# Expert weights loaded in place and split by the Scalar and Vector engines, the slot products cut in two, the spike terms and the first A x V moved: a perceiver block on one core

## The reference, cut to what matters

```python
x = x + cross_attention(layernorm(x), ctx, mask, Wq, Wkv, Wo, qn_w, kn_w)
# self block, per sequence of 32 tokens:
Q, K, V = (sigmoid(4 * (batchnorm(xn @ W) - 1)) for W in (Wq, Wk, Wv))
t_Q, t_K = 1 - mean(Q), 1 - mean(K)
d = t_Q - t_K.T
A = where(d < 0, f, -f) + 0.9        # f = 0.9 * exp(-|d| / 0.5)
x = x + A @ V @ Wo + bo
# experts: 8 of them, the best 2 per token; w1, w3 (8, 512, 256), w2 (8, 256, 512)
scale = top-2 of softmax(xn @ gate_w)
x = x + sum_e (silu(scale * xn @ w1[e]) * (scale * xn @ w3[e])) @ w2[e]
```

## Time and profile before

| what | us |
| --- | --- |
| median of 3 runs | 832.8 (831.76, 832.80, 837.01) |
| the profiled execution, its own time | 832.88 |
| its span, from the first to the last instruction | 831.1 |
| PE busy in 200 to 300 us, cross attention | 100.00 of 100 |
| PE busy in 580 to 600, z stage | 15.78 of 20 |
| PE busy in 620 to 630, AO stage | 7.27 of 10 |
| PE busy in 670 to 680, routing | 3.62 of 10 |
| PE busy in 740 to 760, slot loop | 20.00 of 20 |

### The profile page before, as it was taken

One profiled execution on the slowest core, in us unless ns is written; L12 is line 12 of the kernel. 1 busy time (PEld: TensorE's weight loads), 2 busy tenths in 40 slices (PEclk: granted clock), 3 DMA queues, 4 the chain that ended last, 5 costly groups with the idle time before them and its releaser, 6 DMA issues.

```text
span 831.1 us, 13413 instructions
## 1 busy us (share of the span) xinstructions
PE 742.9 (89%) x4437; PEld 646.0 (78%) x4437; DVE 542.2 (65%) x1022; ACT 492.6 (59%) x1078; POOL 263.9 (32%) x184
## 2 busy tenths in 40 slices
PE   5899999999999999999999977999798728999960
PEld 3688899999999998989999966787577627788840
DVE  6876786868867768677686767634655563544532
ACT  4766785867767767678576663453274324566540
POOL 2561221212121212122121144626647122656530
PEclk9999999999999999999999999899998958999995
DMA  9831212111212212121213041120217652666658
GB/s 307 62 111 39 76 44 72 56 58 41 73 38 76 76 38 76 38 76 38 66 48 119 9 111 55 67 87 9 93 63 232 225 192 73 111 109 112 105 72 304
DMA packets 60039, 75.97 MB, mean 91 GB/s; under 512 B 8768, under 2 KB 33344, under 8 KB 60000
## 3 DMA queue, kind: packets, MB, share of 16 engines
q1 hardware_dynamic: 52544, 59.21, 23.8%
q0 software_dynamic: 5152, 12.06, 8.2%
q10 hardware_dynamic: 2304, 4.20, 1.4%
HBM read 54.75 MB, written 20.71 MB: 91 GB/s over the span
## 4 chain that ended last, share of the span: by engine, by line
PE 77%; DVE 9%; DMA 5%; ACT 4%; POOL 2%; issue 2%; SPq 1%; DVEq 0%; POOLq 0%; ACTq 0%
PE pK L32 35%; PE pV L32 12%; PE pP L32 10%; PE pS L32 6%; PE pT L1453 3%; PE pT L1634 3%; PE pP L1617 2%; DMA fin<-total 1%; PE pT L1739 1%; DMA total<-big,idx 1%; DVE a_flat L1226 1%; DMA big<-x_rows,idx_x 1%; PE pS L1688 1%; DVE bst L939 1%; DMA bn_vec<-in_L_attn_vv_dram 1%
## 5 line engine op out<-in xcount | busy, mean ns | idle before, releaser
L32 PE MATMUL pK<-parts 128*128 128x512 f32 x840 | 213.0, 402 | 7.9 <-POOL parts L512 7.9
L481 POOL TENSOR_TENSOR parts<-big,parts 128x1024 fp32r<-128x1024 f32 x32 | 77.4, 2418 | 340.7 <-ACT parts L710 340.7
L32 PEld LDWEIGHTS pK<-parts 128*128 128x128 f32 x840 | 153.9, 190 | 37.3 <-POOL parts L512 8.4
L32 PE MATMUL pK<-w,lhs 128*128 x276 | 71.2, 408 | 1.4 <-DVE lhs L1381 1.1
L32 PEld LDWEIGHTS pK<-w,lhs 128*128 128x128 f32 x276 | 51.9, 195 | 12.7 <-issue 2.6
L1402 DVE TENSOR_TENSOR w_p<-big,w_p 128x1024 fp32r<-128x1024 f32 x23 | 28.2, 1225 | 51.1 <-ACT w_p L902 48.7
L981 DVE TENSOR_TENSOR kn<-pK,head_rs 128x512 f32<-128x512 f32 x62 | 42.7, 688 | 20.1 <-ACT head_rs L612 19.5
L32 PE MATMUL pS<-kT,qblk 128*128 128x258 f32 x384 | 52.4, 287 | 2.0 <-DVE qoT L1015 2.0
L738 ACT ACTIVATE pT<-pP 128x512 fp32r<-128x512 f32 x32 | 19.1, 598 | 56.8 <-PE pP L1617 56.8
L32 PE MATMUL pP<-pT,parts 128*128 128x256 f32 x384 | 51.9, 284 | 0.0
L32 PEld LDWEIGHTS pS<-kT,qblk 128*128 128x128 f32 x384 | 49.1, 193 | 2.3 <-DVE qoT L1015 2.3
(11 more groups left out here) (273 smaller groups left out, 1597.6 us busy)
## 6 DMA issues: line engine op xcount, KB each, us to landing
big<-in_ctx_dram SPq DMA_DIRECT2D x32, 512.0 KB, 3.8
big<-in_L_ffn_w_dram SPq DMA_DIRECT2D x24, 512.0 KB, 4.8
total<-zero SPq DMA_DIRECT2D x32, 256.0 KB, 3.9
fin<-total SPq DMA_DIRECT2D x8, 512.0 KB, 7.2
big<-in_L_xattn_Wkv_dram SPq DMA_DIRECT2D x2, 1024.0 KB, 10.8
x_rows<-xn ACTq DMA_DIRECT2D x8, 256.0 KB, 2.3
total<-big ACTq DMA_DIRECT2D x8, 256.0 KB, 2.8
out_dram<-fin SPq DMA_DIRECT2D x4, 512.0 KB, 6.5
```

The costliest lines, as they stand in the source:

```text
L32: last = pe.matmul(out, lhs(a, c), rhs(b, c), start=start and c == first and n == 0, stop=stop and c == chunks - 1 and n == 2)
L481: nc.gpsimd.tensor_tensor(ctxN[:, u, LO], ctx_raw[:, u], ctxN[:, u, HI].bitcast(F32), ALU.subtract).then_inc(cn_lo, 1)
```

## The change

- **Layout.** Each expert's w1 and w3 land where its low part will be (`w13_raw[e]`), and the low part is written over them. For this `xT` moves to 64 KB, the self block's weights to their own `w_a` at 96 KB, `xn3` into the region of `w_raw` and `a_flat` over `bn_vec`.
- **Loads.** SP loads experts 0 and 1 behind the second set of `bn_vec`, 2 behind the third, 3 when 16 tiles of z are through, 4 to 6 when all of z is, 7 behind the last product with Wo. All of w2 is loaded at once when x and its normed copy are stored.
- **Splits.** POOL does none for the experts. ACT makes the high parts of 0, 1, 2 at n = 4, 6, 8, of 3 at n = 20, of 4 to 6 in halves at s = 1 to 6, of 7 after the routing. DVE makes the low parts of 0, 1, 2 at n = 6, 8, 10, of 3 at n = 22, of 4 to 6 in quarters, two in each of s = 2 to 7, of 7 in quarters in the first four slots.
- **Spike terms.** The diagonal matrices are written by ACT, two at each of n = 10 to 13; `ones` holds 1/512, so that the factor is in the product, which PE does right behind `z_product(15)`. d and |d| come at n = 17, exp at n = 18, A at n = 19 and 20.
- **First A x V** ahead of `z_product(23)`, its split at n = 22 and 23.
- **Routing.** The 24 row values get their own 16 products (24 columns), and `idx_x` is made ahead of the gates', which follow with 48 columns. POOL gathers before it waits for `zeroed` and `x2_out`.
- **Slot loop.** The last two results are copied into `xg`'s buffers, without the wait for a scatter; the last split of w2 comes behind that slot's hidden tile; the expert's number is loaded ahead of the waits.

```diff
...
-        a_flat = at("a_flat", [P, 2 * D], 60 * KB)
-        xT = at("xT", [P, 2, C, TILES * P], 96 * KB, F32R)
-        xn3 = at("xn3", [P, TILES, D], 112 * KB)
+        a_flat = at("a_flat", [P, 2 * D], 128 * KB)
+        xT = at("xT", [P, 2, C, TILES * P], 64 * KB, F32R)
+        w_a = at("w_a", [P, 2, 2, C, D], 96 * KB, F32R)
+        xn3 = wide[:, 0:2 * C * D].rearrange("p (t d) -> p t d", t=TILES)
...
+        w13_raw = [at(f"w13_raw{e}", [P, C, D], (2 * e + 1) * 8 * KB) for e in range(E)]
...
+        p_slot = pV1[:, 0:NJ]
+        p_gates = pP_flat[:, 0:2 * NJ].rearrange("p (v j) -> p v j", v=2)
...
+            return y_sb[:, j % 2, :] if j < NS - 2 else xg[:, j % 2, :]
...
+            def load_expert(e):
+                if e >= 4:
+                    sp.wait_ge(w13_hi, e - 3)
+                for lo, w in ((0, w1), (F, w3)):
+                    sp.dma_start(w13_raw[e][:, :, lo:lo + F], chunked(w[e])).then_inc(w13_in[e % 4], 16)
...
                 if w == 1:
-                    load_weight("av", "aq")
-
+                    sp.wait_ge(o_mm, 2 * TILES)
+                    load_expert(0)
+                    load_expert(1)
+            sp.wait_ge(xo_mm, TILES)
+            load_expert(2)
+            load_weight("av", "aq")
             load_weight("ao", "ak")
...
+            sp.wait_ge(z_c, 2 * TILES)
+            load_expert(3)
+            sp.wait_ge(z_mm, 3 * TILES)
+            for e in (4, 5, 6):
+                load_expert(e)
+            sp.wait_ge(ao_mm, TILES)
+            load_expert(7)
...
+            sp.wait_ge(xn_out, 16 * TILES)
...
-                if e >= 4 and e % 2 == 0:
-                    sp.wait_ge(w13_last, e // 2 - 1)
...
-            nc.gpsimd.memset(ones[:, :], 1.0)
+            nc.gpsimd.memset(ones[:, :], 1.0 / D)
...
-            for i in range(6):
-                w13_low(i)
...
                 gather(j)
+            pool.wait_ge(zeroed, 16 * B)
+            pool.wait_ge(x2_out, 16 * TILES)
...
+            def w13_high(e, part=slice(0, C)):
+                act.wait_ge(w13_in[e % 4], 32 * (e // 4 + 1))
+                act.activation(w13[:, e, HI, part], w13_raw[e][:, part], ACT.Copy).then_inc(w13_hi, 1)
...
+                if n in (4, 6, 8):
+                    w13_high(n // 2 - 2)
+                if TILES + 2 <= n < TILES + 6:
+                    for t in (2 * (n - TILES - 2), 2 * (n - TILES - 2) + 1):
+                        act.wait_ge(bn_c, 3)
+                        act.activation(a_all[:, t, :], ident[:, :], ACT.Copy, scale=rows[:, 0, t:t + 1]).then_inc(t_act, 1)
+                if n == 3 * TILES - 4:
+                    w13_high(3)
                 if n == 3 * TILES - 2:
-                    w13_high(0)
-                if n == 2 * TILES + 4:
-                    act.wait_ge(t_step, TILES + 4)
+                    self_high(0)
+                if n == 2 * TILES + 2:
+                    act.wait_ge(t_step, 4)
                     act.activation(a_flat[:, :], a_flat[:, :], ACT.Exp, scale=-1.0 / TAU).then_inc(t_act, 1)
...
-                if s < 5:
-                    w13_high(s + 1)
+                if 1 <= s <= 6:
+                    w13_high(4 + (s - 1) // 2, slice(2 * ((s - 1) % 2), 2 * ((s - 1) % 2) + 2))
...
-            w13_high(6)
             w13_high(7)
...
+                if 2 <= j < NS - 2:
                     act.wait_ge(added[j % 2], 16 * (j // 2))
-                act.activation(y_sb[:, j % 2, :], pY[j % 2], ACT.Copy).then_inc(y_set, 1)
+                elif j >= 2:
+                    act.wait_ge(xg_t, NS)
+                act.activation(y_of(j), pY[j % 2], ACT.Copy).then_inc(y_set, 1)
...
+                if i == NS:
+                    w2_high(NS - 1)
...
+                if i < NS - 1:
...
+            def w13_low(e, part=slice(0, C)):
+                dve.wait_ge(w13_hi, e + 1 if e < 4 else 11 if e == 7 else 2 * e - 4 + part.start // 2 + 1)
+                tt(w13[:, e, LO, part], w13_raw[e][:, part], w13[:, e, HI, part].bitcast(F32),
+                   ALU.subtract).then_inc(w13_last if e == 7 else w13_lo, 1)
...
-                    for r in range(TILES):
-                        ts(a_all[:, r, :], ident[:, :], rows[:, 0, r:r + 1], 1.0 / D, ALU.mult,
-                           ALU.mult).then_inc(t_step, 1)
                     ts(rows[:, 1, :], rows[:, 1, :], 1.0 / D, None, ALU.mult).then_inc(t_step, 1)
-                if n == 2 * TILES + 4:
+                if n == 2 * TILES + 1:
 
                     dve.wait_ge(t_pe, 1)
-                    dve.wait_ge(t_step, TILES + 1)
+                    dve.wait_ge(t_step, 1)
                     for g in range(2):
...
+                    dve.wait_ge(t_step, 3)
                     stt(a_all[:, :, :], dt_all[:, :, :], -1.0, dt_all[:, :, :], ALU.mult, ALU.max).then_inc(t_step, 1)
...
+                if n == 2 * TILES + 3:
+
+                    dve.wait_ge(t_step, 4)
                     ts(dt_all[:, :, :], dt_all[:, :, :], 0.0, 2 * A_STDP, ALU.is_lt, ALU.mult).then_inc(t_step, 1)
-                    dve.wait_ge(t_step, TILES + 5)
-                    dve.wait_ge(t_act, 1)
+                    dve.wait_ge(t_step, 5)
+                    dve.wait_ge(t_act, TILES + 1)
                     stt(dt_all[:, :, :], dt_all[:, :, :], -A_STDP, a_all[:, :, :], ALU.add, ALU.mult).then_inc(t_step, 1)
-                    dve.wait_ge(t_step, TILES + 6)
+                if n == 2 * TILES + 4:
+
+                    dve.wait_ge(t_step, 6)
                     stt(dt_all[:, :, :], dt_all[:, :, :], W_OFF, same_seq[:, :].unsqueeze(1).broadcast_to([P, TILES, P]),
...
+                if n in (6, 8, 10):
+                    w13_low(n // 2 - 3)
+                if n == 3 * TILES - 2:
+                    w13_low(3)
+                if n == 3 * TILES - 1:
+                    self_low(0)
...
+                if 2 <= s < TILES:
+                    for c in (2 * (s % 2), 2 * (s % 2) + 1):
+                        w13_low(4 + (s - 2) // 2, slice(c, c + 1))
...
-            routed(tt(tile_val[:, :, :, :], tile_hot[:, :, :].unsqueeze(2).broadcast_to([P, TOP_K * TILES, 3, NJ]),
-                      r_val[:, :, :].bitcast(F32).unsqueeze(3).broadcast_to([P, TOP_K * TILES, 3, NJ]), ALU.mult), val_set)
+            routed(tt(tile_val[:, :, 0, :], tile_hot[:, :, :],
+                      r_val[:, :, 0].bitcast(F32).unsqueeze(2).broadcast_to(pairs), ALU.mult), val_set)
...
+            gates = [P, TOP_K * TILES, 2, NJ]
+            routed(tt(tile_val[:, :, 1:3, :], tile_hot[:, :, :].unsqueeze(2).broadcast_to(gates),
+                      r_val[:, :, 1:3].bitcast(F32).unsqueeze(3).broadcast_to(gates), ALU.mult), val_set)
...
+            dve.wait_ge(i_mm, 1)
+            routed(tt(idx[:, :], p_slot, slot_row[:, :], ALU.add))
+            after_step()
+            routed(ts(idx_x[:, :], idx[:, :], T - 1, None, ALU.bitwise_and), idx_set)
...
-            dve.wait_ge(i_mm, 1)
-            routed(tt(idx[:, :], p_slot[:, 0, :], slot_row[:, :], ALU.add))
-            after_step()
-            routed(ts(idx_x[:, :], idx[:, :], T - 1, None, ALU.bitwise_and), idx_set)
-            routed(nc.vector.tensor_reduce(gate_of[:, :], p_slot[:, 1:3, :].rearrange("p v j -> p j v"), AX.X, ALU.add), idx_set)
+            dve.wait_ge(i_mm, 2)
+            routed(nc.vector.tensor_reduce(gate_of[:, :], p_gates.rearrange("p v j -> p j v"), AX.X, ALU.add), idx_set)
...
-            w13_low(6)
-            w13_low(7)
...
+                if i == NS:
+                    w2_low(NS - 1)
+                if i < C:
+                    w13_low(E - 1, slice(i, i + 1))
...
+                if n == 3 * TILES - 1:
+                    pe.wait_ge(t_step, 7)
+                    self_product(0)
...
-                if n == 2 * TILES + 1:
-                    pe.wait_ge(t_step, TILES)
+                if n == 2 * TILES - 1:
+                    pe.wait_ge(t_act, TILES)
...
-                last = pe.matmul(p_slot, row_hot[:, k, :], tile_val[:, k], start=k == 0, stop=k == pairs - 1)
+                last = pe.matmul(p_slot, row_hot[:, k, :], tile_val[:, k, 0, :], start=k == 0, stop=k == pairs - 1)
+            last.then_inc(i_mm, 1)
+            pe.wait_ge(val_set, 4)
+            for k in range(pairs):
+                last = pe.matmul(p_gates, row_hot[:, k, :], tile_val[:, k, 1:3, :], start=k == 0, stop=k == pairs - 1)
             last.then_inc(i_mm, 1)
...
-                    pe.wait_ge(w13_lo, 6)
-                    pe.wait_ge(w13_last, 2)
+                    pe.wait_ge(w13_lo, 4 + 3 * C)
+                if j == E:
+                    pe.wait_ge(w13_last, C)
...
```

117 lines of the change are left out of this document (39 added, 78 removed).

## The result

| | before | after |
| --- | --- | --- |
| median of 5 runs | 832.46 us (831.44 to 837.01) | 810.85 us (806.96 to 813.14) |
| ratio, 95% interval | | 0.973 [0.9691, 0.977] |
| profiled execution, its span | 831.1 | 805.2 |

The forecast was 811.5, with a range of 806 to 820. Each boundary is a row of the profile; a stretch is the difference of two.

The account below looks back on a forecast made before the run. PE's waits between the K tiles and the routing were taken as mostly DVE held up by POOL. Savings of 16.0 (z gap and AO stage), 2.0, 2.3 and 1.0 made 21.3 off 832.9: 811.6, stated as 811.5, range 806 to 820.

Parts of the forecast that it names:

- The z gap: Behind `z_product(15)`: three z products and the product by `ones` fall from 17.2 us to 9.8, saving 7.4.
- The AO stage: From the z gap to the routing: 10.6 us of waits and slow products regained, less 2.0 of new costs.
- Routing: From the routing's first step to `idx_x`: narrower index products bring `idx_x` 2.0 us earlier, bounds 0.8 and 2.6.
- Gathers: Second gather, no longer beside w2's loads, lands in 4.7 instead of 7.02: 2.3 us saved, bounds 0 and 2.7.
- First slots: First four slots: DVE's extra quarter against its value load moved off the path, together taken as 0.
- SP's queue: SP's expert loads around the third `bn_vec` and in the z stage: four more megabytes, costed at nothing.
- The end: Last slots: 0.7 us from making `hT` before the last w2 split, 1.0 with the copy's scatter wait; bounds 0 and 2.6.
- DVE as the bound: AO stage: DVE sets the pace, six tiles take 6.0 instead of 4.97, +6 us, 817.5; chance 0.13.
- POOL still holding DVE: Low part at n = 10 and four terms of A held up beside POOL's work: 814.5; chance 0.10.
- Gathers sharing with w2: The gathers still share with w2's loads, so the 2.3 us is lost: 814; chance 0.12.
- A late load: ACT waits at a `w13_high` ahead of a sigmoid; one transfer of about 5 us shows once: 816.5; chance 0.06.
- a clock that stays down: Short waits keep PE at 1.2 GHz over the AO stage and 20 us more: 841, slower than before; chance 0.03.

Follow-up runs that it names:

- diag_dve1: Changed kernel with the eight diagonal matrices back on DVE, the product by `ones` behind `z_product(17)` and the terms of A one tile later: 817.33 us.
- pool_low1: Changed kernel with the low parts of experts 4 to 6 made whole by POOL in the AO stage instead of DVE's quarters: 810.67 us.
- sp_late: Changed kernel with the loads of expert 2 and Wv held back until the third `bn_vec` set has landed: 808.82 us, ratio 0.9705 to before.
- best: Changed kernel with `sp_late`'s wait, expert 7's low part whole ahead of the first `x_low`, and unread products in PE's idle time: 808.05 us, ratio 0.9699.
- again1: The changed kernel profiled and timed once more with no edit: 811.28 us, span 809.4.
- warm1: Changed kernel with unread products added in PE's idle time: three before the members, six before the `row_hot` products, two before the first slot's transposes: 808.72 us.

## Why the prediction was right, point by point

The time, 811.5 against 810.85, and the sum, 21.3 against a difference of 21.6 between the medians, are right. The mechanism on which 16.0 of the 21.3 rest, PE waiting for a DVE that POOL holds up, is right too. Of the seven terms the z gap is right, the AO stage right in size with its condition misnamed, the end right in sum with its parts exchanged; the other four miss in both directions and cancel.

- **The z gap, 7.4.** Measured 7.2, and `diag_dve1` puts it back. The product by `ones` took 1.88 and no wait was in front. DVE's terms of A, costed at 0.5, did grow beside POOL (1.83, 2.12 and 1.72, where `diag_dve1` has 1.30, 1.23 and 1.22, the last two with POOL quiet) and were hidden. POOL was held in its turn: its eight adds of bo took 11.51 in place of 9.92.
- **The AO stage, 10.6 less 2.0, with the gap 16.0.** Measured 16.6 and 14.9. The wait for the first `lhs2` is 1.03 for 1.1; the wait of 1.64 for the last tile is there to the digit; tiles are 4.97 to 5.0. The 0.4 and the 0.5 don't show. What the forecast didn't see is that the wait of 1.64 can bring the clock down behind it, which makes 1.7 between two profiles of one kernel. And its sentence "POOL is out of the AO stage now, so the 3.88 goes back to 0.55" names the wrong condition. POOL may stay, as `pool_low1` shows, if its pieces don't meet a norm.
- **Routing, 2.0.** Measured 0.84, at the lower bound of 0.8. The step that failed is "between a third of 0.226 and the whole of it, I take 0.12, near the lower end because the weight load stays". If the weight load is the reason, the upper end follows from it and not the lower: 24, 48 and 72 columns cost 3.59, 3.59 and 3.62. The 0.84 is nearly all DVE's smaller product ahead of them, 1.36 to 0.56.
- **Gathers, 2.3.** Measured 4.4. The cause named, w2's loads beside them, is right and is worth 4.2 alone. The term was mis-sized in two places: the second gather, taken at 4.7, lands in 3.6 (659.91 to 663.5), and its start behind `idx_x` comes 1.3 sooner, since POOL's first gather takes 1.28 in place of 2.59. That 2.59 stood in the earlier trace rows and wasn't asked about; it is DVE's hold on POOL.
- **First slots, 0.** 1.0 to 1.3 were gained: the clock is back at 1.00 in the window of 668 to 670, 3 us after the first product's start, where before it was 0.82 in the window that begins 4 us after it; the product takes 4.41 or 4.14 in place of 5.20. Not all of it is the change's: in the nine profiles whose gathers run as here that product takes 3.93 to 4.94. The 0.7 to 0.9 of the later slots are two slots that took 5.51 and 5.01 before, where the others take 4.8.
- **SP's queue, 0.** 1.2 lost at the third `bn_vec`, shown by `sp_late`. "Their condition is met earlier" was true of experts 0 and 1; the loads that did harm are those right behind the third `bn_vec`.
- **The end, 1.0.** Measured 1.07, with the parts exchanged: 0.7 for the order is 0.1, and the buffers, for which 0.3 was left, are 1.1. PE's earlier end alone buys nothing, since the copy then stands at the scatter.
- **The rivals.** DVE as the bound: out, since taking a third of its work away (`pool_low1`) gains nothing. POOL still holding DVE: seen in the terms of A, hidden. Gathers sharing with w2: not here, but `best` shows that it was 2 us away. A late load, and a clock that stays down: no. The 841 of that rival is a slip in the sum: by its own words, 39.8 us become 80, it is over 851.
- **The signs.** The product by `ones`, the first `lhs2`, the tiles, the norms (0.55 at most) and the second gather are as forecast. The clock of 1.00 up to the routing is so in the first profile and not in `again1`. The first slot's product is 23.0 us earlier than 688 there and 18.1 in `again1`, whose part ahead of the z gap took 1.9 longer than before; so that sign asked for more than the change decides.

Forecast too high were the routing by 1.2, the queue by 1.2 and, in `again1`, the stage by 1.1; too low were the gathers by 2.1 and the slots by some 2. That the sum came out within a microsecond was luck in its parts.

## What to carry to other kernels

Between DVE and GpSimd ask not how much work they share but what meets what: in these traces an operation that reads PSUM or takes statistics passes, a norm from SBUF to SBUF waits until GpSimd's piece ends, a gather's issue on GpSimd waits until DVE's subtraction ends, and a start moved by nearly 4 us was worth 10. When a stage ahead of a gather gets faster, look at which bulk load was just out of its way. And a term that comes out right in sum should be split once by experiment, since its halves may be exchanged.

## What was unexpected

- A wait of PE of 1.64 us ended with the 16 gate products behind it at 1.97 in one profile and at 3.42 in another, of one kernel. One product put into it (`best`, wait 0.68) gave 1.97; that was one profile.
- Products of 24, 48 and 72 columns cost the same: 0.224 each at a granted clock of 0.50 and 0.121 to 0.137 at 1.00.
- After the 32 small products of `warm1`, with PE's busy time at 2.00 of 2, the clock fell to 0.57 in 660 to 662 all the same. Why isn't settled.
- Two megabytes issued right behind the four small loads of `bn_vec` made these land in 6.5 in place of 5.3.
- A DVE subtraction of two SBUF operands lengthened GpSimd's issue of a gather from 1.28 to 2.35.
